# Layer 2 of a decoder kernel: half 1 tile by tile up to its transform, another order of products and perceptron, weight parts later on GpSimd

## The reference

```python
scores = jnp.einsum('bthd,bghd->bhtg', Q, K) / np.sqrt(DH).astype(np.float32)
topv, topi = jax.lax.top_k(scores, K_TOP)                    # K_TOP = 32
probs = jax.nn.softmax(topv, axis=-1)
attn = jnp.zeros_like(scores).at[bi, hi, ti, topi].set(probs)
attn_mean = attn.mean(axis=1)
c_t = jnp.einsum('btg,bgd->btd', attn_mean, V)
x = layernorm(x_text, g_norm_in, b_norm_in)
scale_in, shift_in = jnp.split(c_t @ W_film_in + b_film_in, 2, axis=-1)
x = x * (1.0 + mod_gate * scale_in) + mod_gate * shift_in
y = s4d(x, log_dt, A_re, A_im, C_re, C_im, D_skip)           # irfft(rfft(x) * rfft(K)) + x * D_skip
scale_out, shift_out = jnp.split(c_t @ W_film_out + b_film_out, 2, axis=-1)
y = y * (1.0 + mod_gate * scale_out) + mod_gate * shift_out
xt = x_text + y
h = layernorm(xt, g_ffn, b_ffn)
xt = xt + jax.nn.gelu(h @ W1 + b1, approximate=False) @ W2 + b2
return layernorm(xt, g_norm_out, b_norm_out)
```

## Time and profile before

| | us |
|---|---|
| median of 3 runs | 658.26 |
| lowest, highest | 658.0, 660.03 |
| the profiled execution | 665.67 |
| its span, first to last instruction | 663.8 |
| busy: TensorE, VectorE | 469.6, 447.7 |
| busy: ScalarE, GpSimd | 267.1, 230.1 |

### The profile page before, as it was taken

One profiled execution on the slowest core, in us unless ns is written; L12 is line 12 of the kernel. 1 busy time (PEld: TensorE's weight loads), 2 busy tenths in 40 slices (PEclk: granted clock), 3 DMA queues, 4 the chain that ended last, 5 costly groups with the idle time before them and its releaser, 6 DMA issues. The chain is left out here.

```text
span 663.8 us, 11995 instructions
## 1 busy us (share of the span) xinstructions
PE 469.6 (71%) x4136; PEld 362.2 (55%) x4136; DVE 447.7 (67%) x1480; ACT 267.1 (40%) x657; POOL 230.1 (35%) x265
## 2 busy tenths in 40 slices
PE   4798226474598859997849577877698885988840
PEld 2376213454477548775726566755377652687730
DVE  4879778989474776654673988985667463145535
ACT  5699511110023435552024555542375121155521
POOL 4132921536432004554010441410563137025540
PEclk9889757696799868997978667989799978899985
DMA  8100033100000040840000000000915001500112
GB/s 284 40 3 1 1 105 150 35 0 1 0 1 1 0 126 4 173 82 0 1 0 1 1 1 1 2 0 2 368 66 132 2 13 55 132 21 33 38 45 87
DMA packets 27966, 33.38 MB, mean 50 GB/s; under 512 B 4945, under 2 KB 21057, under 8 KB 27394
## 3 DMA queue, kind: packets, MB, share of 16 engines
q1 hardware_dynamic: 25970, 29.13, 15.0%
q0 software_dynamic: 1504, 3.15, 1.4%
q10 hardware_dynamic: 432, 0.33, 0.2%
HBM read 26.44 MB, written 6.16 MB: 49 GB/s over the span
## 5 line engine op out<-in xcount | busy, mean ns | idle before, releaser
L1789 POOL TENSOR_TENSOR ea_scaled_rows<-ea_scaled_rows 128x768 f32<-128x768 f32 (+2 forms) x24 | 27.8, 1157 | 61.5 <-ACT ea_scaled_rows L1716 60.3
L3205 POOL DMA_INDIRECT em_results<-em_y_slot,slot_rows x31 | 29.8, 960 | 50.7 <-DVE em_y_slot L3336 42.4
L219 ACT ACTIVATE norm_log<-norm_var 128x4 f32<-128x4 f32 x20 | 4.1, 204 | 81.7 <-DVE norm_var L197 81.5
L3092 PE MATMUL banks<-em_slotT,em_weights 128*128 128x128 f32 x248 | 33.5, 278 | 4.3 <-ACT em_weights L2967 3.7
L3327 DVE SCALAR_TENSOR_TENSOR em_innerT<-banks,em_bias_of,em_soft 128x128 f32<-128x128 f32 x62 | 18.8, 345 | 25.2 <-ACT em_soft L3151 23.5
L2355 POOL TENSOR_TENSOR ga_to_end<-ga_cum 128x512 f32<-128x512 f32 x8 | 12.4, 1546 | 65.1 <-DVE ga_cum L2411 65.0
L1716 ACT ACTIVATE ea_scaled_rows<-banks,ea_gate 128x192 f32<-128x192 f32 x64 | 23.5, 419 | 25.5 <-PE banks L38 25.4
L3092 PEld LDWEIGHTS banks<-em_slotT,em_weights 128*128 128x128 f32 x248 | 30.1, 192 | 6.3 <-issue 6.3
L3151 ACT ACTIVATE em_soft<-banks,em_bias_of 128x128 f32<-128x128 f32 x62 | 19.6, 374 | 26.4 <-remote 17.4
L2742 POOL TENSOR_TENSOR ca_prob<-ca_prob,ca_most 128x1232 f32<-128x1232 f32 x8 | 18.0, 2249 | 19.6 <-DVE ca_most L2795 19.6
L3104 PE MATMUL banks<-em_down,em_innerT 128*128 x124 | 19.5, 281 | 7.4 <-DVE em_innerT L3327 7.4
(11 more groups left out here) (505 smaller groups left out, 1530.4 us busy)
## 6 DMA issues: line engine op xcount, KB each, us to landing
em_up<-in_em_up SPq DMA_DIRECT2D x3, 1536.0 KB, 11.5
ea_wide<-ea_gates SPq DMA_DIRECT2D x4, 1024.0 KB, 16.6
em_down<-in_em_down SPq DMA_DIRECT2D x3, 768.0 KB, 12.8
em_slots<-slot_rows SPq DMA_DIRECT2D x1, 2108.0 KB, 11.0
w_qkv<-in_w_qkv SPq DMA_DIRECT2D x1, 1536.0 KB, 7.1
slot_rows<-em_slots SPq DMA_DIRECT2D x1, 1360.0 KB, 8.0
cos_lag<-in_cos_lag SPq DMA_DIRECT2D x1, 1024.0 KB, 5.5
sin_lag<-in_sin_lag SPq DMA_DIRECT2D x1, 1024.0 KB, 7.8
```

What stands on the lines that cost most here:

```text
L1789: step(pool.tensor_tensor(scaled_rows[:, k, 0:n], scaled_rows[:, k, 0:n], scaled_rows[:, k, n:2 * n], ALU.add))
L3092: ins = pe.matmul(s.ps[:, k * P:(k + 1) * P], weights[:, n % NW, k // 2, k % 2 * P:(k % 2 + 1) * P], slotT[:, n], start=True, stop=True, s ...
L3205: pool.indirect_dma_start(core.results[:, :], bass.IndirectOffsetOnAxis(ap=slot_rows[:, s, P:P + 1].bitcast(U32), axis=0), y_slot[:, s % N ...
```

## The change

Half 1 no longer goes as a whole. For tiles 4 to 7 there are single steps: `mean_tile`, `film_tile` (context and FiLM product of one tile) and `forth_tile`, which adds one tile's part to `xr1` and `xi1`. The mean and the FiLM product of tile 4 stand ahead of `forth(0)`, those of 5 and 6 behind it, and `forth_tile(4)` between the mean and the FiLM product of tile 7. ScalarE copies tile by tile (`context_of_tile`), and VectorE does `film_of(g)` and `scale(g)` tile by tile.

For the last tile, 7, VectorE takes over GpSimd's `shift`, `weigh` and `average` (`shift_last`, `average_last`). VectorE's `multiply(0)` stands between these two, `multiply(1)` and `combine(1)` stand ahead of `modulate(0)`, and the products of half 1 have two buffers of their own (`parts_of`).

TensorE then runs `back(0)`, `back(1)`, `up(0)`, `up(1)`, `down(0)`, `down(1)`. On ScalarE the root for half 1's `modulate` stands ahead of `gelu(0)`, and the copy of `hT1` behind it; one return to the first table is left out. On GpSimd `add_bias(1)` and then a wait for all of `h` stand ahead of the three `low_part`.

```diff
-part = [sb(f"part{n}", [P, LT, P]) for n in range(4)]
-yr, yi = part[0], part[2]
+part = [sb(f"part{n}", [P, LT, P]) for n in range(6)]
+parts_of = [part[0:4], [part[4], part[1], part[5], part[3]]]
...
-order = [("mean", 0), ("film", 0), ("forth", 0), ("mean", 1), ("back", 0), ("film", 1), ("back_end", 0),
-         ("forth", 1), ("up", 0), ("back", 1), ("back_end", 1), ("down", 0), ("up", 1), ("down", 1)]
-for stage, b in order[:3]:
-    plan += work[b][stage]
+order = [("mean", 0), ("film", 0), ("mean_tile", 4), ("film_tile", 4), ("forth", 0), ("mean_tile", 5),
+         ("film_tile", 5), ("mean_tile", 6), ("film_tile", 6), ("mean_tile", 7), ("forth_tile", 4),
+         ("film_tile", 7), ("forth_tile", 5), ("forth_tile", 6), ("forth_tile", 7), ("back", 0), ("back", 1),
+         ("up", 0), ("up", 1), ("down", 0), ("down", 1)]
+plan += ["meanT0", "c0"] + [f"film{g}" for g in range(HT)] + ["xr0", "xi0"]
 ring.update(core.ring.plan(plan, (7, 0, 1, 2)))
-ring.update(core.ring.plan([n for stage, b in order[3:] for n in work[b][stage]], (3, 4, 5, 6, 0, 1, 2, 7)))
+ring.update(core.ring.plan(["xr1", "xi1"], (0, 1)))
+plan = []
+for g in range(HT, NT):
+    plan += [f"mean_tile{g}", f"c_tile{g}", f"film{g}"]
+ring.update(core.ring.plan(plan, (3, 4, 5, 6)))
+plan = [f"y{b}" for b in range(B)]
+for b in range(B):
+    plan += [f"hT{b}"] + [f"up{b}{j}" for j in range(4)]
+plan += [f"down{b}" for b in range(B)]
+ring.update(core.ring.plan(plan, (2, 7, 3, 4, 5, 6, 0, 1)))
...
+        def mean_of_tile(g):
+            s = ring[f"mean_tile{g}"]
+            s.claim(pe)
+            pe.wait_ge(mean_ready, g + 1)
+            pe.transpose(s.ps[0:G, 0:P], mean[:, g], ident[:, :]).then_inc(s.filled, 1)
+
+        def film_of_tile(g):
+            ring[f"mean_tile{g}"].taken(pe)
+            s = ring[f"c_tile{g}"]
+            s.claim(pe)
+            pe.matmul(s.ps[:, 0:P], v[:, g // HT], meanT[:, g], start=True, stop=True).then_inc(s.filled, 1)
+            s.taken(pe)
+            film_product(g)
...
+        def forth_of_tile(g):
+
+            i = g % HT
+            pe.wait_ge(u_ready, 2 + i)
+            for name, w in (("xr1", t["cos_half"]), ("xi1", t["sin_half"])):
+                s = ring[name]
+                if i == 0:
+                    s.claim(pe)
+                for f in range(LT):
+                    ins = pe.matmul(s.ps[:, f * P:(f + 1) * P], w[:, i, f * P:(f + 1) * P], u[:, g],
+                                    start=(i == 0 and f == 0), stop=(i == LT - 1), skip_group_check=True)
+                if i == LT - 1:
+                    ins.then_inc(s.filled, 1)
...
+        def context_of_tile(g):
+            move(f"mean_tile{g}", meanT[:, g], lambda s: s.ps[0:G, 0:P])
+            move(f"c_tile{g}", cT[:, g], lambda s: s.ps[:, 0:P])
...
-        for g in range(5, NT):
-            exp(g)
-        context(1)
+        exp(5)
+        context_of_tile(4)
+        exp(6)
+        context_of_tile(5)
+        exp(7)
+        context_of_tile(6)
+        context_of_tile(7)
...
         core.norm.act(act, step)
         move("hT0", hT[:, half(0)])
+        core.norm.act(act, step)
         ring["b1"].taken(act)
         gelu(0)
-        load_exp_and_log(act)
-        core.norm.act(act, step)
         move("hT1", hT[:, half(1)])
-        core.norm.act(act, step)
         gelu(1)
         load_exp_and_log(act)
-        for _ in range(2 * B - 1):
+        for _ in range(2 * B):
...
-        for g in range(NT):
+        for g in range(NT - 1):
             weigh(g)
             if g == 5:
                 scale(0)
-            if g + 1 < NT:
+            if g + 1 < NT - 1:
...
         add_bias(0)
-        pool.wait_ge(y_ready, 2 * B)
+        add_bias(1)
+        pool.wait_ge(h_ready, NT)
         for n in range(3):
             pool.wait_ge(core.rounded, n + 3)
             low_part(pool, columns(core.w_low, n), columns(t["w_qkv"], 3 + n), columns(core.w_high, n)
                      ).then_inc(core.w_split, 1)
-        add_bias(1)
...
+        def film_of(g):
+            s = ring[f"film{g}"]
+            s.ready(dve)
+            dve.scalar_tensor_tensor(film[:, g].rearrange("p k c -> p (k c)"), s.ps[:, :], rows["mod_gate"],
+                                     film_const[:, :, :, :].rearrange("p o k c -> p (o k c)"),
+                                     ALU.mult, ALU.add).then_inc(s.drained, 1)
+
+        def scale(g):
+            ring[f"film{g}"].taken(dve)
+            dve.wait_ge(normed, g // HT + 1)
+            step(dve.tensor_tensor(u[:, g], u[:, g], film[:, g, 0], ALU.mult))
+            dve.tensor_tensor(u[:, g], u[:, g], film[:, g, 1], ALU.add).then_inc(u_ready, 1)
+
+        def shift_last():
+
+            k = (NT - 1) % 2
+            dve.wait_ge(mean_ready, NT - 2)
+            dve.tensor_tensor(prob[:, k], score[:, k], spread(top[:, k, 0, :, 0], 2, [P, H, G]),
+                              ALU.subtract).then_inc(shifted, 1)
+
+        def average_last():
+
+            k = (NT - 1) % 2
+            dve.wait_ge(selected, NT)
+            dve.wait_ge(exps, NT)
+            step(dve.scalar_tensor_tensor(prob[:, k], left[:, k], SELECTED, prob[:, k], ALU.is_equal, ALU.mult))
+            step(dve.tensor_reduce(total[:, k], prob[:, k], AX.X, ALU.add))
+            step(dve.reciprocal(total[:, k], total[:, k]))
+            step(dve.tensor_scalar(total[:, k], total[:, k], text_weight[:, NT - 1:NT], None, ALU.mult))
+            step(dve.tensor_tensor(prob[:, k], prob[:, k], spread(total[:, k], 2, [P, H, G]), ALU.mult))
+            step(dve.tensor_tensor(prob[:, k, 0:2], prob[:, k, 0:2], prob[:, k, 2:4], ALU.add))
+            dve.wait_ge(mean_ready, NT - 1)
+            dve.tensor_tensor(mean[:, NT - 1], prob[:, k, 0], prob[:, k, 1], ALU.add).then_inc(mean_ready, 1)
...
+            part = parts_of[b]
...
-        for g in range(NT):
-            if g + 1 < NT:
-                select(g + 1)
+        for g in range(NT - 1):
+            select(g + 1)
             if g == 2:
                 s = ring["b1"]
                 s.ready(dve)
                 dve.tensor_tensor(b1[:, :], s.ps[:, 0:4], bias["xa_b1"], ALU.add).then_inc(s.drained, 1)
-            if g == NT - 1:
-                multiply(0)
             invert(g)
             if g == 3:
                 norm_in(1)
             if g == 4:
-                film_of(0)
+                for n in range(HT):
+                    film_of(n)
+            if g == 5:
+                film_of(4)
+        shift_last()
+        multiply(0)
+        average_last()
         combine(0)
-        film_of(1)
-        scale(1)
-        modulate(0)
+        scale(4)
+        for g in range(5, NT):
+            film_of(g)
+            scale(g)
         multiply(1)
         combine(1)
+        modulate(0)
         modulate(1)
```

56 lines of the change are left out of this document (18 added, 38 removed).

## The result

The changed kernel took 672.53 us (median of 4 runs, 666.48 to 674.73); the kernel before, with one more run beside its three, 659.14 (658.0 to 663.76). The ratio is 1.0143, interval 1.0095 to 1.0191: slower by some 1.4%. (A ratio is estimated from the single runs, without any that lies in the chip's slower state, over 1.5% above the fastest of its kernel; it is not the quotient of the medians, which is 1.0203 here, and I give both.) The prediction said 660.7, at most 662.9. The direction was right and the time was not: by the medians +13.4 us, by the ratio +9.4, where +2.5 was forecast.

What follows compares the result with a forecast made beforehand. TensorE was taken to bound layer 2 from 176 to 210 us, then VectorE's normalisations. Head -7.5 and tail +10.0 gave +2.5 us on the median of 658.26, about 660.7; range 657.5 to 662.9.

Steps and rivals of the forecast that it cites:

- VectorE ahead of the hinge: Layer 2, VectorE's added work before combine(0): film_of(4) 0.66, shift_last 0.4, average_last 0.36 us more; combine(0) at 174.97.
- the hinge: Layer 2, where TensorE ends half 1's inverse transform and VectorE reads it, at 210.31 us before the change.
- upper bound of 3.7: Layer 2, the last average on VectorE: 3.7 us at GpSimd's time for its last three operations, against the 2.4 taken.
- The wait for bank 4: Layer 2, tile 7's transpose waits until VectorE has run film_of(5), 0.7 us more; forth_tile(4) starts at 177.85.
- The low clock in the head: Layer 2 before D: TensorE's clock stays low for 3.4 us of work after idling, costing 1.7 us.
- Rival (d): More waits in the chain by tiles: VectorE +1.3, ScalarE round trip +0.7, longer low clock +1.7; 662 to 664 us; chance 0.10.
- D: Time of the hinge in layer 2: forecast 202.8 us, 7.5 us earlier than before the change.
- Tail: Layer 2 after D: 15.8 + 9.9 + 9.6 us plus 1.4 for low clock, 36.7; 10.0 us longer than 26.7.
- Edits costed at nothing: GpSimd's moved weight parts (3.73 us), half 1's bias, two more buffers and keep_busy ending earlier: no cost.
- Rival (c): ScalarE's table switch also costs a drain of about 1380 ns: 1.4 us more, 662.1 us; chance 0.04.
- The sum: Layer 2's -7.5 and +10.0 us give +2.5 on the median of 658.26, about 660.7 us.
- rival (b): Clearly faster: later stages fall differently on the clock's switches, half of 5 us saved, 655.5 us; chance 0.09.

Runs made afterwards that it cites:

- warm head: The changed kernel with dummy matmuls in TensorE's idle time of layer 2, ahead of the transposes for tiles 6 and 7: 643.23 us, ratio 0.9973 to the kernel before.
- after_third: The changed kernel measured a third time, unchanged, against the kernel before: 647.38 us, ratio 1.0036.
- after_fourth: The changed kernel measured once more, unchanged, against the kernel before: 648.53 us, ratio 1.0047.
- warm4_after: The changed kernel with three dummy matmuls at the start of layer 4: 645.75 us, ratio 1.0018 to the kernel before.
- after_again: The changed kernel measured again, unchanged, against the kernel before on another chip than the first: 647.46 us, ratio 1.0027.
- up_between: The changed kernel with half 0's perceptron between the inverse transforms, back(0) early, modulate(0) ahead of multiply(1), ScalarE's old order: 643.02 us, ratio 0.9979 to the kernel before.
- new_tail: The kernel before with only the change's order behind the inverse transforms (TensorE, ScalarE, GpSimd): 654.56 us, ratio 1.0137 to the kernel before.

## Why the prediction was right and wrong

**VectorE ahead of the hinge: right.** `combine(0)` was forecast at 174.97 and starts at 173.67, that is 174.95 with the 1.28 us by which the layer began earlier. The last average takes 2.5 us (171.16 to 173.67), forecast 2.4; its upper bound of 3.7 wasn't needed. The wait for bank 4, read off the order, is there with 2.16 us, and the forward transform starts at 177.9 (176.62 + 1.28) where 177.85 was forecast.

**The low clock in the head: the step that failed in layer 2.** I wrote "I take the low level again: half of 3.4 us is 1.7". It lasted 8.4 us under the work, which is 4.2 us. (The rows of before show some 3.2, not 3.4.) Rival (d) had "a low clock for twice as long (+1.7)"; it was +2.5. D was forecast 7.5 us earlier and came 5.25, 6.4, 5.1 and 5.5 us earlier in four profiles of after. By my own test, "D lies outside 201 to 204", the recorded 203.78 would pass, but only because layer 1 had ended earlier: with 1.28 added it is 205.06, and the head failed. The warm head shows that in the first profile nothing but the clock was missing. What I took from before was the length of a low stretch behind an idle time, and that length is no property of the work. The same code has 8.3 to 8.6 us of it under the work in four profiles (after, after_third, after_fourth, warm4_after) and 3.0 in after_again:

```profile
177.74 1.92 PE L1120 MATMUL banks<-xa_u,cos_half 128*128 128x128 f32 x8
179.45 1.66 PE L1120 MATMUL banks<-xa_u,sin_half 128*128 128x128 f32 x8
180.94 0.39 PE L1093 MATMUL banks<-xa_meanT,xa_v 77*128 77x128 f32 x2
181.68 1.13 PE L1072 MATMUL banks<-xa_wfilm,xa_cT 128*128 128x512 f32 x2 [0.35 <-ACT xa_cT L1180]
```

Nor are gaps in the work needed: without one, `back(0)` of `up_between` has 5.1 us and `back(1)` of `new_tail` 5.3. What decides the length is not shown. In after_again the clock's term was about right and D still came 1.1 us later than forecast, because the forward transform started 1.3 us later since the layer's start than in the first profile: VectorE's `shift_last` did so by 1.2 us, from a cause ahead of the rows read here.

**Tail: right, in size and in each step.** Forecast +10.0, measured +10.1, and +10.1 again in the profile of the new tail alone. `finish(0)` at D + 17.4 was forecast as 15.8 + 1.4, the low clock at `up(1)` included (5.40 us, forecast 5.11). "Near D + 16, after some 9 us" was written without that 1.4: the wait is 11.53 us, and the forecast's own terms give 15.8 + 1.4 - 5.9 = 11.3. The second `finish` has no wait.

**Edits costed at nothing: right.** GpSimd's weight parts run from 209.74 for 3.71 us while VectorE is idle, and `keep_busy` ends at 231.6, well before the layer; layer 3's first microseconds run at the low clock in both kernels.

**Rival (c), a drain at each switch of tables: not here.** ScalarE in after:

```profile
207.72 0.21 ACT L220 ACTIVATE norm_root<-norm_log 128x4 f32<-128x4 f32 x1
207.94 1.28 ACT L1204 ACT_TABLE_LOAD   x1
209.24 2.42 ACT L1204 ACTIVATE far<-banks,xa_b_moved 128x512 f32<-128x512 f32 x4
```

The load starts 0.01 us behind the root, takes 1.28, and the Gelu starts 0.02 us behind it: no idle time on either side. The Trainium skill ("ScalarE: Activation LUTs", What ACT_TABLE_LOAD costs) has a drain of about 1380 ns there; this trace shows none.

**The sum.** Layer 2 was forecast +2.5 and is +4.9, +3.8, +5.1 and +4.6 in four profiles against the first one of before; the miss is the head's, by the clock's term in three of them and by the later start in after_again. The kernel's times, +1.7 to +3.4 us in the three later measurements, lie around the forecast of +2.5, partly because the untouched layers 1 and 3 took 1.3 to 2.6 us less together in the four profiles of after than in the first of before. Nothing in the forecast says so, and that part of the agreement is luck. Layer 3's part of it goes with the clock again: some 70 us into that layer the clock stays low for 6.8 us in the profile of before and in after_again (101.87 and 101.98 us), and for 3.4 us in the other three of after (100.5). Two sums of the prediction are off by their own terms, without bearing on the result: rival (b)'s 655.5 should be 655.2 (657.7 less half of 5), and 2 to 5 us of low clock each time would be +1.4 to +4.4, not +0.8 to +3.6.

**The 10 us beyond it: the step that failed for the kernel's time.** It is "I read that layer and took the rest as it is", with the forecast added to the median of before; rival (b) had the loss in words only. "All later stages fall differently on the clock's switches ... It can as well lose that": I gave this 2.5 us and a chance on the gain's side only. One stage can hold 8.4 us of it. A range that took this in would have reached 670 without a word on the change itself. This explains the distance of the two profiles, 9.1 us. That of the medians, 13.4, it doesn't explain in full: the profile of before was itself 6.5 us above its median, by a cause that I found in no row before and have not found since. Also open is why three of the first four runs lay at 670.7 to 672.9 us of span, when none of the 34 later ones lies 5 us above its median. Only the profiled one has a trace, and that the others had the same stretch is inferred from their mean clocks (0.842 and 0.839 beside 0.838). The fourth, 666.48, is still 7.3 us above before's median, and no trace says why. In the four profiles of after the first rise in layer 4 came 12.9, 14.2, 20.8 and 44.8 us after the layer's start, for the same code; I can't say what decides it.

## What to carry over

A kernel's untouched stages can move its time by more than the edit does, so price an edit from its own layer in the trace, and ask for a second measurement on another chip before explaining a surprise in the median. Behind an idle time of TensorE, give the low clock a range and not the one length that a profile of before has: 3.0 to 8.6 us of it lay under the work here, for one and the same code. A few dummy matmuls in the wait are a cheap test of that term. When two halves are reordered, what counts is which work still lies beside the last stage: half 0's `finish` beside half 1's products was worth 10 us here, more than the whole gain of the finer head.
